# First keys placed from two queues, and the second group's queries and keys made after the first scores

## The chip, the cores and the metric

The kernel runs on one core of one Trainium2 chip. The metric is device microseconds of one execution. The engines are PE (TensorE: matmuls, and PEld for its weight loads), DVE (VectorE), ACT (ScalarE), POOL (GpSimd) and SP (SyncE, which only issues transfers). Each engine runs its own instructions in order and waits on semaphores; SP, ACT and POOL issue DMAs from their own queues.

## What is computed

A window-attention block followed by a gated depthwise-convolution block, on `x` of shape (8, 64, 32, 32), all in float32. The change touches only the start of the first block:

```python
xn = _layernorm(xc, ln1_scale, ln1_bias)              # over channels
qkv = xw @ w_qkv + b_qkv                              # windows of 8x8 pixels, 8 heads, depth 8
attn = jnp.einsum('bnhd,bmhd->bhnm', q * scale, k)
attn = attn + bias.transpose(2, 0, 1)[None]           # relative position bias from a small table
attn = jax.nn.softmax(attn, axis=-1)
out = jnp.einsum('bhnm,bmhd->bnhd', attn, v)
```

## The kernel before

The image columns are cut into NG = 8 groups of 512 columns (G), each NW = 8 windows. A group passes through these stages; the number in brackets is the line in the kernel before.

- The input is split into a high and a low part (`high_of_x`, `low_of_x` [L550, L287]), centred on PE (`centered` [L787]), squared on ACT (`square_of_centered` [L555, L556]), the square split again (`low_of_square` [L287]), averaged on PE (`variance` [L787]), turned into 1/deviation on ACT (`inverse_deviation` [L561, L563]) and multiplied in on DVE (`normalise` [L1194]).
- PE makes keys, queries and values (`keys` [L809], `queries` [L814], `values` [L819]). ACT evacuates their high parts (`evacuate_k` [L572], `evacuate_q` [L581]) and DVE makes the low parts (`k_low` [L1198], `q_low` [L1203]).
- The evacuated parts are spread by DMA into block layouts: `spread_keys` [L379] and `spread_queries` [L391] on SP, 8 DMAs each (the queries twice a group, one half after the other), and `first_key_blocks` [L453] and `query_blocks` [L469] on POOL, 4 DMAs each. `k_heads` and `q_heads` also hold rows of the position bias, written once: the keys' by `bias_with_keys` [L1172], the queries' early half by `bias_with_queries` [L1180] on DVE, the late half by `late_bias` [L675] on ACT. They come from two loaded tables, `rel_flipped` and `rel_table`, through `high_of_bias` [L1185] and `low_of_bias` [L1190].
- A first pass of products per window (`scores_for_max` [L840]) gives DVE the row maxima (`take_maximum` [L1216]), in three PSUM banks. They are transposed (`transpose_maxima` [L846]) and negated (`spread_maxima` [L1222 to L1225]); then `scores` [L864, L867] starts its sum with minus the maximum (through the constant `pick` [L435]), and ACT takes the exponentials (`exponentials` [L601]).

`step(g, ...)` holds the scores of group g, mixed with values and the pass for the maxima of the next group, and with centring, keys and queries of the one after. Ahead of `step(0)` each engine has a start-up written out by hand, and that is where the change lies. Nothing schedules the order: each engine's list is the order of the code, and semaphores tie the lists. SP's start-up is `spread_keys(0)`, both halves of `spread_queries(0)`, `spread_keys(1)`, four loads of `x`, and then 24 DMAs a group.

Of the kernel before, what the change touches and what calls it, by code (L numbers as in the profile page):

```python
# [7 lines left out]
WS, NH, HD = 8, 8, 8  # L8
# [90 lines left out]
def conv_seq_kernel(nc, d, out):  # L99
# [4 lines left out]
    with ctx:  # L104
# [105 lines left out]
        def gate_memory(space, nb):  # L210
# [22 lines left out]
            "ac_sq", "ac_log", "ac_rstd", "ac_q_high", "ac_k_high", "ac_v", "ac_probs", "ac_proj", "ac_sq2", "ac_log2", "ac_rstd2",   # L233
            "dv_normed", "dv_k_low", "dv_q_low", "k_heads_in", "q_blocked", "q_blocks_in", "k_blocked", "k_blocks_in", "q_heads_in0", "q_heads_in1", "dv_max", "dv_maxt", "dv_minus", "dv_turned", "dv_inv", "dv_ratios", "dv_att", "dv_x1", "dv_normed2",
            "pe_mlp1", "pe_mlp2", "pe_pw1", "ac_gelu", "ac_relu", "dv_x2", "dv_hsum",
# [94 lines left out]
        def query_rows(part, half, windows):  # L330
            rows = of_half(q_heads[:, part], half).rearrange("p h (w t) -> p h w t", t=T)
            return rows[:, :, windows.start:windows.stop, :]

        QUADRANTS = [(hh, bh, slice(hh * 64 + bh * 32, hh * 64 + bh * 32 + 32)) for hh in range(2) for bh in range(2)]

# [4 lines left out]
        def _(sp):  # L340
# [25 lines left out]

            def of_head(t, h):
                first = h // (NH // 2) * 64 + h % (NH // 2)
                return t[first:first + 64 - NH // 2 + 1:NH // 2]
# [12 lines left out]
            def spread_queries(n, half):  # L382

                if n == 0:
                    sp.wait_ge(S[f"q_heads_set{half}"], 1 + half)
# [44 lines left out]
        def _(pool):  # L430
            pool.memset(k_blocks[:, :, :, 1].bitcast(F32).rearrange("p h s w t -> p (h s) (w t)"), 0.0).then_inc(S["k_blocks_zeroed"], 1)
            pool.memset(gaps[:], 0.0).then_inc(S["zeroed"], 1)
            pool.wait_ge(S["consts_in"], 16)
            pool.wait_ge(S["center_in"], 16)
            pool.tensor_tensor(pick[:], const("average").unsqueeze(1).to_broadcast([128, NW, 128]),  # L435
# [11 lines left out]
            def first_key_blocks():  # L447

                pool.wait_ge(S["k_blocks_zeroed"], 1)
                pool.wait_ge(S["k_blocks_set"], 1)  # L450
                pool.wait_ge(S["dv_k_low"], 1)
# [32 lines left out]

            low_of_next_x(1)
            first_key_blocks()
            low_of_next_square(1)
# [44 lines left out]
        def _(act):  # L532
# [32 lines left out]
            def evacuate_k(n, par):  # L565
                act.wait_ge(S["pe_k"], n + 1)
                if not (isinstance(n, int) and n < 2):
                    act.wait_ge(S["k_heads_in"], 16 * NH * (n - 1))
                    act.wait_ge(S["k_blocks_in"], 64 * (n - 1))
# [85 lines left out]
            act.wait_ge(S["eps_set"], 1)  # L655
            act.dma_start(weights[:, _WAT["vec"][1]:], d["weights"][:, _WAT["vec"][1]:]).then_inc(S["weights_in"], 16)
            inverse_deviation(0)
            act.wait_ge(S["consts_in"], 16)
            for half in range(2):
                ins = act.activation(k_blocks[:, half, :, 0], reversal().rearrange("p (s w) t -> p s w t", s=2), ACT.Copy, scale=not_in_half(half))  # L660
            ins.then_inc(S["k_blocks_set"], 1)
            act.wait_ge(S["x_in0"], 32)
            high_of_x(1)
            act.wait_ge(S["qkv_ready"], 1)
            evacuate_k(0, 0)
            evacuate_q(0, 0)
# [5 lines left out]
            def late_bias(part, rel):  # L672
                late = range(NW // 2, NW)
                for half in range(2):
                    ins = act.activation(query_rows(part, half, late), bias_rows(rel, half, late), ACT.Copy, scale=not_in_half(half))  # L675
                ins.then_inc(S["q_heads_set1"], 1)

            act.wait_ge(S["dv_rel_low"], 1)
            late_bias(0, rel_high)
            inverse_deviation(1)  # L680
            act.wait_ge(S["x_in1"], 32)
            high_of_x(2)
            late_bias(1, rel_low)
            evacuate_q(1, 1)
            evacuate_k(1, 1)
            act.wait_ge(S["weights_ready"], 1)
# [96 lines left out]
        def _(pe):  # L783
# [39 lines left out]
            def scores_for_max(n, w):  # L823

                if w == 0:
                    if isinstance(n, int) and n == 0:
                        pe.wait_ge(S["q_blocked"], 1)
                    else:
                        pe.wait_ge(S["q_blocks_in"], 64 * n)
                    pe.wait_ge(S["k_heads_in"], 16 * NH * (n + 1))  # L830
                elif w == 1:
# [83 lines left out]
            def step(g, nxt, far, prev, par):  # L915
# [4 lines left out]

                scores(g, 0)
                if nxt is not None:
                    values(nxt)
# [39 lines left out]
            queries(0)  # L963
            values(0)
# [3 lines left out]
            pe.matmul(psum[:, PV, 5:6], proj_raw, qkv_bias[:, 2:3], start=True, stop=True).then_inc(S["pe_biases"], 1)  # L968
            centered(1)
# [161 lines left out]
        def _(dve):  # L1131
# [481 lines left out]
```

## Time and profile before

| | |
|---|---|
| median of 3 runs | 326.47 us (326.3 to 327.18) |
| profiled execution, its own time | 329.44 us |
| its span, first to last instruction | 327.6 us |
| busy: PE, DVE, ACT, POOL | 289.0 us (88%), 246.9 (75%), 203.0 (62%), 92.0 (28%) |
| chain that ended last, shares | PE 61%, DVE 12%, SP's queue 9%, ACT 6%, DMA 4% |
| one maximum on DVE (L1216), mean of 64 | 682 ns |

The chain is followed back from the last instruction, at each step to what released it; an engine busy outside of it costs nothing.

### The profile page before, as it was taken

The page shows a single profiled execution, that of the slowest core. Times are in us where ns is not written, and L with a number is a line of the kernel's source. Part 1 is how long each engine was busy: PE and PEld are TensorE (multiplying, and loading weights), DVE is VectorE, ACT ScalarE, POOL GpSimd, SP SyncE. Part 2 cuts the span into 40 slices and gives each one's busy share as a digit, 9 for nine tenths or more (in the row PEclk, how much of TensorE's full clock was granted, in tenths as well). Part 3 has the DMA queues.
Part 4 walks back from the last instruction along what each step waited for, and adds up shares of the span by engine and source line. Part 5 has one row for each costly group of instructions (what it writes and reads, how often), then busy time and mean ns, then how long its engine had stood idle before and what let it go on. Part 6 is the DMA issues. An engine that isn't in the chain of part 4 may idle for free.

```text
span 327.6 us, 6201 instructions
## 1 busy us (share of the span) xinstructions
PE 289.0 (88%) x2314; PEld 209.9 (64%) x2314; DVE 246.9 (75%) x484; ACT 203.0 (62%) x343; POOL 92.0 (28%) x116
## 2 busy tenths in 40 slices
PE   0577897989999898999979897899899999999994
PEld 0345684768868687776868653354477777777772
DVE  3686589579899898989977354779999999976211
ACT  5587643838658585765735697977961755754500
POOL 4063316255263464534250611131310000000000
PEclk9995999999999999999998999999999999999998
DMA  6961356224132331413320000392007568766911
GB/s 152 179 141 44 79 138 119 57 73 89 34 90 63 72 75 36 103 55 71 74 73 13 2 1 2 65 211 58 0 2 145 126 129 179 142 139 144 191 32 32
DMA packets 16380, 28.10 MB, mean 86 GB/s; under 512 B 5088, under 2 KB 11744, under 8 KB 16352
## 3 DMA queue, kind: packets, MB, share of 16 engines
q1 hardware_dynamic: 13792, 22.72, 30.5%
q0 software_dynamic: 1984, 4.20, 7.3%
q10 hardware_dynamic: 576, 0.81, 1.0%
q8 instruction: 18, 0.29, 0.4%
q14 instruction: 10, 0.08, 0.1%
HBM read 4.22 MB, written 2.10 MB: 19 GB/s over the span
## 4 chain that ended last, share of the span: by engine, by line
PE 61%; DVE 12%; SPq 9%; ACT 6%; DMA 4%; issue 4%; POOL 2%; DVEq 0%; ACTq 0%
PE psum L1088 26%; PE psum L867 8%; SPq L391 5%; PE psum L787 5%; SPq L379 4%; PE psum L1012 3%; DVE maxima L1216 3%; PE psum L864 3%; PE psum L1000 3%; DMA k_heads<-k_parts 3%; POOL parts L287 2%; PE psum L809 2%; PE psum L840 2%; PE psum L883 2%; DVE k_blocks L1210 2%
## 5 line engine op out<-in xcount | busy, mean ns | idle before, releaser
L1088 PE MATMUL psum<-shifted,conv_w 128*128 128x512 f32 x336 | 86.6, 419 | 0.0
L1088 PEld LDWEIGHTS psum<-shifted,conv_w 128*128 128x128 f32 x336 | 63.9, 191 | 21.5 <-issue 1.3
L867 PEld LDWEIGHTS psum<-q_heads,k_blocks 128*128 128x128 f32 x384 | 55.4, 191 | 5.9 <-issue 2.8
L867 PE MATMUL psum<-q_heads,k_blocks 128*128 128x256 f32 x384 | 56.6, 283 | 0.0
L1216 DVE TENSOR_REDUCE maxima<-psum 128x8 f32<-128x512 f32 x64 | 40.4, 682 | 11.1 <-PE psum L840 10.0
L601 ACT ACTIVATE probs<-psum 128x512 f32<-128x512 f32 x64 | 37.4, 603 | 15.8 <-PE psum L867 15.6
L287 POOL TENSOR_TENSOR parts<-x,parts 128x256 fp32r<-128x256 f32 (+1 forms) x21 | 19.4, 938 | 59.2 <-ACT parts L609 33.7
L787 PE MATMUL psum<-parts,center_average 128*128 128x512 f32 x64 | 23.1, 443 | 13.7 <-DVE parts L287 9.4
L864 PE MATMUL psum<-minus_max,pick 128*128 128x512 f32 x64 | 32.3, 504 | 2.4 <-DMA q_heads<-q_parts 1.9
L840 PE MATMUL psum<-k_heads,q_blocks 128*128 128x256 f32 x128 | 23.3, 308 | 8.1 <-DMA k_heads<-k_parts 5.5
L273 ACT CAST conv_w<-conv_w 32x896 fp32r<-32x896 f32 x31 | 29.1, 938 | 0.4
L1476 DVE SCALAR_TENSOR_TENSOR x<-psum,weights,x 64x512 f32<-64x512 f32 x16 | 12.0, 749 | 21.0 <-PE psum L1088 20.9
L287 POOL TENSOR_TENSOR parts<-square_logvar,parts 128x512 fp32r<-128x512 f32 x14 | 18.0, 1287 | 31.3 <-ACT square_logvar L556 16.0
L840 PEld LDWEIGHTS psum<-k_heads,q_blocks 128*128 128x128 f32 x128 | 19.4, 204 | 11.6 <-issue 6.3
L730 ACT CAST conv_w<-whole_w 128x896 fp32r<-128x896 f32 x8 | 7.5, 936 | 27.5 <-DVE whole_w L1451 18.9
L514 POOL TENSOR_TENSOR images<-square_logvar,images 128x512 fp32r<-128x512 f32 x8 | 10.7, 1339 | 42.0 <-ACT images L713 42.0
L787 PEld LDWEIGHTS psum<-parts,center_average 128*128 128x128 f32 x64 | 10.4, 200 | 17.0 <-issue 9.6
L703 ACT ACTIVATE hidden<-psum,mlp_bias 128x512 f32<-128x512 f32 x32 | 19.5, 699 | 2.5 <-PE psum L1000 2.4
L1000 PE MATMUL psum<-normed,mlp_w 128*128 128x512 f32 x64 | 18.4, 425 | 1.4 <-ACT hidden L703 1.4
L883 PEld LDWEIGHTS psum<-probs,v_blocks 128*32 128x32 f32 x1024 | 15.5, 112 | 5.2 <-issue 4.9
L1210 DVE CAST k_blocks<-k_parts 32x512 fp32r<-32x512 f32 x28 | 12.9, 459 | 7.4 <-PE psum L867 7.0
L461 POOL DMA_DIRECT2D k_blocks<-k_parts x28 | 16.1, 583 | 7.4 <-PE psum L867 6.8
(143 smaller groups left out, 486.9 us busy)
## 6 DMA issues: line engine op xcount, KB each, us to landing
shifted<-images SPq DMA_DIRECT2D x32, 332.5 KB, 5.5
q_heads<-q_parts SPq DMA_DIRECT2D x128, 32.0 KB, 1.8
k_heads<-k_parts SPq DMA_DIRECT2D x64, 32.0 KB, 2.3
out<-x SPq DMA_DIRECT2D x8, 256.0 KB, 4.9
q_blocks<-q_parts POOLq DMA_DIRECT2D x28, 64.0 KB, 2.5
k_blocks<-k_parts POOLq DMA_DIRECT2D x28, 64.0 KB
x<-in_x SPq DMA_DIRECT2D x6, 256.0 KB, 5.1
x<-in_x SPq DMA_DIRECT2D x4, 128.0 KB, 4.8
```

The costliest lines, as they stand in the source:

```text
L273: ins = copy(conv_w[bh][shift * KS:(shift + 1) * KS, part, :, C:], w[(shift - 1) * KS:shift * KS, :, 0:C])
L287: return engine.tensor_tensor(low, whole, high.bitcast(F32), ALU.subtract)
L601: act.activation(probs[:, w, :], psum[:, PROB0 + w % 2, :], ACT.Exp).then_inc(S["ac_probs"], 1)
L703: act.activation(hidden[:, par, m, :], psum[:, HIDDEN0 + m, :], ACT.Gelu, bias=mlp1_bias[:, m % 2:m % 2 + 1]).then_inc(S["ac_gelu"], 1)
L787: ins = pe.matmul(psum[:, bank, :], center_average[:, which, :], parts[:, part, :], start=part == 0, stop=part == 1)
L840: ins = pe.matmul(max_bank(w)[:, hh * G // 2:(hh + 1) * G // 2], q_blocks[:, hh, w, :], of_half(k_heads, hh)[:, :, w * T:(w + 1) * T], sta ...
L864: pe.matmul(bank, pick[:, w, :], minus_max[:, :, :], start=True, stop=False)
L867: ins = pe.matmul(bank[:, hh * G // 2:(hh + 1) * G // 2], k_blocks[:, hh, w // (NW // 2), k_part, w % (NW // 2), :], of_half(q_heads[:, q_ ...
L883: ins = pe.matmul(psum[32 * j:32 * j + 32, PV, column:column + T], v_blocks[:, par, at:at + 32], probs[:, w, head * T:(head + 1) * T], sta ...
L1000: ins = pe.matmul(psum[:, HIDDEN0 + m, :], mlp1_w[:, part, f * 128:(f + 1) * 128], normed2[:, bh, bass.ds(n * G, G)], start=part == 0, sto ...
L1088: ins = pe.matmul(psum[:, CONV0 + bh, :], conv_w[bh][:, w_part, t, :], img[:, y:y + H - 1:2, x0:x0 + W], start=t == 0 and w_part + part == ...
L1216: dve.tensor_reduce(maxima[:, w * NH:(w + 1) * NH], max_bank(w).rearrange("p (h t) -> p h t", t=T), AX.X, ALU.max).then_inc(S["dv_max"], 1)
```

## The change

It makes six moves, all at the start.

1. `spread_keys(0)` issues only heads 0 to 3 on SP; POOL issues heads 4 to 7, ahead of `first_key_blocks`, under a semaphore of its own. PE and ACT wait for both.
2. POOL makes `pick` after the first centring on PE and no longer as soon as the constants are in.
3. On DVE, `high_of_bias(1, rel_high)` stands ahead of `normalise(0)`; both biases and both low parts stand before the maxima, with the queries' first, and `other_weights` too; `normalise(1)` stands behind all eight maxima.
4. On ACT, the two halves of the key blocks' constants stand on either side of `inverse_deviation(0)`, one of the four late bias copies ahead of `evacuate_q(0)` and the other three ahead of `inverse_deviation(1)`.
5. On PE, the small bias products stand ahead of `values(0)`, and `variance(1)` behind the sixth window of the first maximum pass instead of the second.
6. `queries(1)` and `keys(1)` are no longer made around `transpose_maxima(0)` but in `step(0)`, behind `scores(0, 0)`; ACT evacuates them behind the first exponential.

```diff
-                for h in range(NH):
-                    sp.dma_start(of_head(k_heads, h)[:, h, :].bitcast(F32).rearrange("p (s c) -> p s c", s=2),
-                                 of_head(k_parts, h)[:, n % 2, :, 0, :].bitcast(F32)).then_inc(S["k_heads_in"], 16)
+                for h in FIRST_KEYS_BY_SP if n == 0 else range(NH):
+                    keys_of_head(sp, n, h, "k_heads_in")
...
             pool.wait_ge(S["consts_in"], 16)
-            pool.wait_ge(S["center_in"], 16)
+            pool.wait_ge(S["pe_xc"], 1)
...
             low_of_next_x(1)
+            pool.wait_ge(S["ac_k_high"], 1)
+            pool.wait_ge(S["k_heads_set"], 1)
+            for h in FIRST_KEYS_BY_POOL:
+                keys_of_head(pool, 0, h, "first_keys_in")
             first_key_blocks()
...
                 exponentials(g, 0)
+                if isinstance(g, int) and g == 0:
+                    evacuate_q(1, 1)
+                    evacuate_k(1, 1)
...
             for w in range(NW):
                 scores_for_max(0, w)
-                if w == 1:
+                if w == 5:
                     variance(1)
-            pe.wait_ge(S["dv_normed"], 2)
-            queries(1)
             transpose_maxima(0)
-            keys(1)
...
             high_of_bias(0, rel_flipped, "dv_rel_flipped")
+            high_of_bias(1, rel_high, "dv_rel_high")
             normalise(0)
             bias_with_keys()
+            low_of_bias()
+            bias_with_queries()
+            q_low(0, 0)
             k_low(0, 0)
-            high_of_bias(1, rel_high, "dv_rel_high")
-            low_of_bias()
-            q_low(0, 0)
-            bias_with_queries()
+            other_weights()
             for w in range(NW):
                 take_maximum(0, w)
-                if w == 3:
-                    normalise(1)
             spread_maxima(0)
-            other_weights()
+            normalise(1)
```

`high_of_bias` waits for its table (`dve.wait_ge(S[f"rel_in{n}"], 32)`) before it copies.

The order on DVE at the start, in the kernel before, from `q_blocks`' constants to the first maxima:

```order
L1167 TENSOR_SCALAR q_blocks<-consts 128x1024 x2
L1185 CAST normed<-probs 128x512
L1194 TENSOR_TENSOR normed<-psum,rstd 128x512
L1172 TENSOR_SCALAR k_heads<-normed,consts 128x2048 x2
L1198 SCALAR_TENSOR_TENSOR k_parts<-psum,qkv_bias,k_parts 128x2x256
L1185 CAST normed<-probs 128x512
L1190 TENSOR_TENSOR normed<-probs,normed 128x512
L1203 SCALAR_TENSOR_TENSOR q_parts<-psum,q_bias,q_parts 128x512
L1180 TENSOR_SCALAR q_heads<-normed,consts 128x4x256 x4
L1216 TENSOR_REDUCE maxima<-psum 128x8 x4
L1194 TENSOR_TENSOR normed<-psum,rstd 128x512
```

The same place on DVE in the changed kernel (L1204 is the copy of a table, L1213 `normalise`, L1222 `q_low`, L1217 `k_low`, L1235 the maxima):

```order
L1186 TENSOR_SCALAR q_blocks<-consts 128x1024 x2
L1204 CAST normed<-probs 128x512 x2
L1213 TENSOR_TENSOR normed<-psum,rstd 128x512
L1191 TENSOR_SCALAR k_heads<-normed,consts 128x2048 x2
L1209 TENSOR_TENSOR normed<-probs,normed 128x512
L1199 TENSOR_SCALAR q_heads<-normed,consts 128x4x256 x4
L1222 SCALAR_TENSOR_TENSOR q_parts<-psum,q_bias,q_parts 128x512
L1217 SCALAR_TENSOR_TENSOR k_parts<-psum,qkv_bias,k_parts 128x2x256
```

Both table copies now stand ahead of the first normalisation, and `k_low` has moved from behind the key bias to behind the query bias.

The order on PE in the kernel before, from the centring of the second group (L787) to the first scores (L864, L867):

```order
L787 MATMUL psum<-parts,center_average 128x512 x2
L840 MATMUL psum<-k_heads,q_blocks 128x256 x4
L787 MATMUL psum<-parts,center_average 128x512 x2
L840 MATMUL psum<-k_heads,q_blocks 128x256 x12
L814 MATMUL psum<-normed,qkv_w 128x512
L846 MATMUL psum<-consts,maxima 64x128
L809 MATMUL psum<-normed,qkv_w 128x512
L864 MATMUL psum<-minus_max,pick 128x512
L867 MATMUL psum<-q_heads,k_blocks 128x256 x6
```

The same place on PE in the changed kernel (L858 is the maximum pass, L864 the transpose, L882 and L885 the scores, L832 and L827 queries and keys):

```order
L805 MATMUL psum<-parts,center_average 128x512 x2
L858 MATMUL psum<-k_heads,q_blocks 128x256 x12
L805 MATMUL psum<-parts,center_average 128x512 x2
L858 MATMUL psum<-k_heads,q_blocks 128x256 x4
L864 MATMUL psum<-consts,maxima 64x128
L882 MATMUL psum<-minus_max,pick 128x512
L885 MATMUL psum<-q_heads,k_blocks 128x256 x6
L832 MATMUL psum<-normed,qkv_w 128x512
L827 MATMUL psum<-normed,qkv_w 128x512
```

The variance has moved from behind two windows to behind six, and queries and keys from ahead of the first scores to behind them.

## Rows read from the trace of the kernel before

**Rows 1.** Timeline of PE: start us, us, engine line operation, xcount [idle before, releaser]

```profile
15.21 2.05 PE L809 MATMUL psum<-normed,qkv_w 128*128 128x512 f32 x2 [2.33 <-DVE normed L1194]
...
26.51 1.20 PE L840 MATMUL psum<-k_heads,q_blocks 128*128 128x256 f32 x4 [4.17 <-DMA k_heads<-k_parts]
27.50 1.05 PE L787 MATMUL psum<-parts,center_average 128*128 128x512 f32 x2
...
33.35 0.43 PE L846 MATMUL psum<-consts,maxima 128*64 128x128 f32 x2 [0.43 <-DVE maxima L1216]
...
35.10 0.47 PE L864 MATMUL psum<-minus_max,pick 128*128 128x512 f32 x1 [0.26 <-issue]
...
49.92 1.10 PE L809 MATMUL psum<-normed,qkv_w 128*128 128x512 f32 x2 [0.19 <-DVE maxima L1216]
...
55.42 0.47 PE L864 MATMUL psum<-minus_max,pick 128*128 128x512 f32 x1 [1.88 <-DMA q_heads<-q_parts]
```

**Rows 2.** Timeline of SP, its DMA issues

```profile
32.67 5.10 SPq L391 DMA_DIRECT2D q_heads<-q_parts  x8
37.86 5.90 SPq L379 DMA_DIRECT2D k_heads<-k_parts  x8
...
46.41 11.37 SPq L391 DMA_DIRECT2D q_heads<-q_parts  x16
```

**Rows 3.** Source line L343 in the window 4 to 6: the second loads of x

```profile
L343 SPq DMA_DIRECT2D x<-in_x x2: 534/565/596, 4.2 to 4.7; - x2
...
DMA to landing us min/median/max: 5.7/6.5/7.2
```

**Rows 4.** Source line L362: the load of the raw weights on SP

```profile
L362 SPq DMA_DIRECT2D probs<-in_raw x1: 560/560/560, 6.7 to 6.7; - x1
...
DMA to landing us min/median/max: 11.3/11.3/11.3
```

**Rows 5.** DMA queue of ACT: packets, MB, share, windows 15:16 and 16:17

```profile
q10 hardware_dynamic: 3, 0.00, 0.3%
...
q10 hardware_dynamic: 29, 0.10, 28.6%
```

**Rows 6.** Timeline of DVE

```profile
5.96 2.46 DVE L287 TENSOR_TENSOR parts<-x,parts 128x256 fp32r<-128x256 f32 x2
...
13.22 0.61 DVE L1185 CAST normed<-probs 128x512 fp32r<-128x512 f32 x1
14.37 0.69 DVE L1194 TENSOR_TENSOR normed<-psum,rstd 128x512 f32<-128x512 f32 x1 [0.53 <-ACT rstd L563]
14.97 2.47 DVE L1172 TENSOR_SCALAR k_heads<-normed,consts 128x2048 fp32r<-128x2048 f32 x2
...
19.39 1.08 DVE L1190 TENSOR_TENSOR normed<-probs,normed 128x512 fp32r<-128x512 f32 x1
...
21.06 2.88 DVE L1180 TENSOR_SCALAR q_heads<-normed,consts 128x1024 fp32r<-128x1024 f32 x4
...
36.10 0.74 DVE L1203 SCALAR_TENSOR_TENSOR q_parts<-psum,q_bias,q_parts 128x512 fp32r<-128x512 f32 x1
```

**Rows 7.** Timeline of POOL

```profile
6.24 1.90 POOL L435 TENSOR_TENSOR pick<-consts 128x1024 fp32r<-128x1024 f32 x1 [3.63 <-DMA consts<-in_consts]
...
19.56 3.23 POOL L453 DMA_DIRECT2D k_blocks<-k_parts  x4 [0.85 <-DVE k_parts L1198]
24.97 1.26 POOL L287 TENSOR_TENSOR parts<-square_logvar,parts 128x512 fp32r<-128x512 f32 x1 [2.18 <-ACT square_logvar L556]
```

**Rows 8.** Timeline of ACT

```profile
17.35 0.69 ACT L572 ACTIVATE k_parts<-psum,qkv_bias 128x512 fp32r<-128x512 f32 x1 [0.41 <-PE psum L809]
```

**Rows 9.** Stretch, PE, PEld, DVE, ACT, POOL busy, PEclk, DMA, GB/s

```profile
24.00:26.00 2.00, 0.00 (x0) 0.00 (x0) 0.00 (x0) 1.98 (x4) 1.03 (x1) 0.64 0.56 105
```

**Rows 10.** Chain that ended last, in order of time: start us, us, what

```profile
172.67 0.73 PE psum L864
173.40 1.28 PE psum L867 x6
174.68 0.32 PE psum L864
175.00 0.71 PE psum L867 x6
```

More of the change, by code:

```diff
@@ L332, in query_rows, with of_head, keys_of_head, wait_keys_placed @@
             return rows[:, :, windows.start:windows.stop, :]
+        def of_head(t, h):
+            first = h // (NH // 2) * 64 + h % (NH // 2)
+            return t[first:first + 64 - NH // 2 + 1:NH // 2]
+        def keys_of_head(engine, n, h, done):
+            engine.dma_start(of_head(k_heads, h)[:, h, :].bitcast(F32).rearrange("p (s c) -> p s c", s=2),
+                             of_head(k_parts, h)[:, n % 2, :, 0, :].bitcast(F32)).then_inc(S[done], 16)
+        FIRST_KEYS_BY_SP, FIRST_KEYS_BY_POOL = range(0, NH // 2), range(NH // 2, NH)
+        def wait_keys_placed(engine, groups):
+            engine.wait_ge(S["k_heads_in"], 16 * (NH * groups - len(FIRST_KEYS_BY_POOL)))
+            engine.wait_ge(S["first_keys_in"], 16 * len(FIRST_KEYS_BY_POOL))
         QUADRANTS = [(hh, bh, slice(hh * 64 + bh * 32, hh * 64 + bh * 32 + 32)) for hh in range(2) for bh in range(2)]
@@ L363, in _ @@
             load_x(1, slice(0, PIX), S["x_in1"])
-            def of_head(t, h):
-                first = h // (NH // 2) * 64 + h % (NH // 2)
-                return t[first:first + 64 - NH // 2 + 1:NH // 2]
             def spread_keys(n):
@@ L377, in spread_keys @@
                     sp.wait_ge(S["pe_max"], NW * n)
-                for h in range(NH):
-                    sp.dma_start(of_head(k_heads, h)[:, h, :].bitcast(F32).rearrange("p (s c) -> p s c", s=2),
-                                 of_head(k_parts, h)[:, n % 2, :, 0, :].bitcast(F32)).then_inc(S["k_heads_in"], 16)
+                for h in FIRST_KEYS_BY_SP if n == 0 else range(NH):
+                    keys_of_head(sp, n, h, "k_heads_in")
             def spread_queries(n, half):
                 if n == 0:
-                    sp.wait_ge(S[f"q_heads_set{half}"], 1 + half)
+                    sp.wait_ge(S[f"q_heads_set{half}"], 1 + 3 * half)
                 else:
@@ L449, in first_key_blocks @@
                 pool.wait_ge(S["k_blocks_zeroed"], 1)
-                pool.wait_ge(S["k_blocks_set"], 1)
+                pool.wait_ge(S["k_blocks_set"], 2)
                 pool.wait_ge(S["dv_k_low"], 1)
@@ L567, in evacuate_k @@
                 if not (isinstance(n, int) and n < 2):
-                    act.wait_ge(S["k_heads_in"], 16 * NH * (n - 1))
+                    wait_keys_placed(act, n - 1)
                     act.wait_ge(S["k_blocks_in"], 64 * (n - 1))
@@ L656, in _, with key_block_constants, late_bias @@
             act.dma_start(weights[:, _WAT["vec"][1]:], d["weights"][:, _WAT["vec"][1]:]).then_inc(S["weights_in"], 16)
+            def key_block_constants(half):
+                act.activation(k_blocks[:, half, :, 0], reversal().rearrange("p (s w) t -> p s w t", s=2), ACT.Copy, scale=not_in_half(half)
+                               ).then_inc(S["k_blocks_set"], 1)
+            def late_bias(part, rel, half):
+                late = range(NW // 2, NW)
+                act.activation(query_rows(part, half, late), bias_rows(rel, half, late), ACT.Copy, scale=not_in_half(half)
+                               ).then_inc(S["q_heads_set1"], 1)
+            act.wait_ge(S["consts_in"], 16)
+            key_block_constants(0)
             inverse_deviation(0)
[L658 to L661, printed above, removed]
+            key_block_constants(1)
             act.wait_ge(S["x_in0"], 32)
@@ L665, in _ @@
             evacuate_k(0, 0)
+            act.wait_ge(S["dv_rel_high"], 1)
+            late_bias(0, rel_high, 0)
             evacuate_q(0, 0)
@@ L670, in _ @@
             square_of_centered(1)
[L672 to L676, printed above, removed]
+            late_bias(0, rel_high, 1)
             act.wait_ge(S["dv_rel_low"], 1)
-            late_bias(0, rel_high)
+            for half in range(2):
+                late_bias(1, rel_low, half)
             inverse_deviation(1)
@@ L682, in _ @@
             high_of_x(2)
-            late_bias(1, rel_low)
-            evacuate_q(1, 1)
-            evacuate_k(1, 1)
             act.wait_ge(S["weights_ready"], 1)
@@ L829, in scores_for_max @@
                         pe.wait_ge(S["q_blocks_in"], 64 * n)
-                    pe.wait_ge(S["k_heads_in"], 16 * NH * (n + 1))
+                    wait_keys_placed(pe, n + 1)
                 elif w == 1:
@@ L921, in step @@
                 scores(g, 0)
+                if isinstance(g, int) and g == 0:
+                    pe.wait_ge(S["dv_normed"], 2)
+                    queries(1)
+                    keys(1)
                 if nxt is not None:
@@ L963, in _ @@
             queries(0)
-            values(0)
             pe.wait_ge(S["raw_in"], 16)
@@ L968, in _ @@
             pe.matmul(psum[:, PV, 5:6], proj_raw, qkv_bias[:, 2:3], start=True, stop=True).then_inc(S["pe_biases"], 1)
+            values(0)
             centered(1)
```

2 lines of the change are left out of this document (1 added, 1 removed).

## The prediction, on record before the changed kernel ran

> **What bounds the kernel now.** I read four views, in this order. The page's chain shows PE for most of the span, so from the middle on the kernel is a PE-led rhythm that this change does not touch; it can only shift it. The chain in order of time then shows that from about 33 to 66 us the shift is set by SP's queue. In its timeline [rows 2] the second half of the first queries is issued from 32.67, the second group's keys from 37.86 and the next 16 queries from 46.41, each block right behind the last (four loads of x stand between the last two). PE's timeline shows who waits for it: at 55.42 it had been idle 1.88 us for q_heads [rows 1]. So the quantity to follow is when SP begins the second group's keys: 37.86 before. What leads up to it is PE's 4.17 us wait for the first keys until 26.51, the transpose of the maxima at 33.35 and the first scores at 35.10 [rows 1]. Last, DVE's timeline shows the start-up's own chain: table copy at 13.22, `normalise(0)` at 14.37, PE's keys at 15.21 [rows 1, 6].
>
> **The table copy ahead of `normalise(0)`.** This edit decides the case. `high_of_bias(1)` waits for rel_table, and DVE is in order, so `normalise(0)` and all behind it wait too. Before, that copy stood late and nothing shows a wait. The landing itself has no row, so I bound it. SP issues rel_table after the second loads of x and before the raw weights. The former was issued last at 4.7 and took up to 7.2: 11.9 us [rows 3]. The latter was issued at 6.7 and took 11.3: 18.0 us [rows 4]. In between, ACT's queue moved 3 packets from 15 to 16 us and 29 from 16 to 17 [rows 5]: something in front of it on the crowded DMA engines was over at about 16, and only rel_table's large rows and the raw weights stood there. I take 16.5, nearer the later bound. The copy costs 0.6 [rows 6], so `normalise(0)` starts at 17.15 and not at 14.37: 2.8 us late. PE's keys go from 15.21 to 18.0.
>
> **What that hides.** Moving `pick` off the start helps: DVE's split of the first x took 2.46 us for two halves while POOL ran `pick` from 6.24 for 1.90 [rows 6, 7], some 1.6 us more than two undisturbed halves by my estimate. The first centring comes that much earlier, but `normalise(0)` then waits for the table anyway: worth 0 at a landing of 16.5, and about 1.0 were the table there. The Trainium skill, SBUF — State Buffer, section SBUF: two separate sides, has DVE and GpSimd share a port pair as an exclusive lock that the first to start holds for its whole instruction. The trace agrees with it in these two rows, and by it the moved `pick` meets the low part of the first square instead, which is why I count 1.0 and not 1.6 there. The key-block constant put ahead of `inverse_deviation(0)` lies in ACT's wait for the variance: 0.
>
> **From `normalise(0)` to the transpose.** DVE now runs without a gap: normalise 0.69, key bias 2.47, low of the table 1.08, query bias 2.88, `q_low` and `k_low` 0.74 each [rows 6], less five overlaps of some 0.06: `k_low` ends at 25.4. Behind it POOL issues the four key-block DMAs, 3.23 us, and only then splits the second square, 1.26 [rows 7]: with 0.3 to start, 30.2. PE has `variance(1)` behind window 5, so it waits until then, takes 0.9 to 1.05, and windows 6 and 7 queue behind it at 0.6 each [rows 1], with a maximum of 0.68 behind each. The transpose T comes at 30.2 + 0.9 + 0.7 + 2 x 0.68 = 33.2, against 33.35. DVE's own eight maxima, begun at about 26.6 behind `other_weights`, would be over by 32.1, so they do not set it. The first keys, the wait of 4.17, are thus moved earlier against their own start, since four issues leave SP, but what they release is not late any more; the gain is given back to the table. If PE's clock is at its full level here, T is 32.6 (lower bound); if the key-block DMAs take the short 0.6 each, 0.5 earlier still.
>
> **From the transpose to SP.** Before, the scores came 1.75 us behind T [rows 1]. Now queries and keys are behind them. At full clock the scores take 1.03 [rows 10], queries 1.03, keys 1.10 [rows 1], ACT's evacuation 0.7 [rows 8] and the handover 0.05: SP can start the second keys at T + 5.65 = 38.85. SP is free by then (the late bias copies end at about 31, its half of the queries takes 5.10 [rows 2]: 36.2). Against 37.86 that is 1.0 late. The removed work does not come back as gain: queries and keys took the wait for `spread_maxima` before, and now cost some 2.1 us between the first scores and the rest of step 0. PE's path there arrives 1.9 us late at the second maximum pass, but had 1.88 us of idle at 55.42 in front of the next scores [rows 1], so SP's 1.0 rules. Behind 66 us everything shifts alike. Edits of which I see no effect: the bias products ahead of `values(0)` (ACT is still copying query blocks), `other_weights` (hidden behind the first landing), POOL's four DMAs if they land by 27.
>
> The sum is +1.0 us. Against the profiled execution, 329.44 us with a span of 327.6, that is 330.4; its own time lies 3 us above the median of the runs, and the same +1.0 on 326.47 gives 327.5.
>
> **Rivals.**
> 1. *The table lands early: faster.* Each microsecond that it lands earlier moves T and SP alike. Break-even is 15.5 us. At 12.9 or before, where the deviation is ready, the whole design works: T at about 29.5, SP at 35.15, 2.7 us gained, 323.8. For it: over half of the range between the two landings [rows 3, 4] lies below 15.5. Against: the packets of ACT's queue [rows 5]. ACT now issues its large load some 1.6 us earlier too, which can only delay it. Chance 0.15.
> 2. *PE's clock falls in front of the first scores: clearly slower.* Before, PE stood idle 4.17 us and the granted clock went to 0.64 of a stretch in which it did nothing [rows 9], so that the pass ran at 1.2 GHz; queries and keys then kept it busy up to the scores. Now they are gone from there: between the variance and the scores PE has two windows and a transpose, under 2 us of work in 4. At the lower level the six score matmuls take 1.28 for 0.71 [rows 10] and the keys 2.05 for 1.10 [rows 1]. For scores, queries and keys that makes +0.6 +0.9 +0.95 = 2.4, straight onto SP's start: +3.4, 329.9. Against it: PE was idle 1.88 us at 55.42 and its scores then took 0.47 as before [rows 1]. Chance 0.27. The Trainium skill, TensorE: Matmul & The Clock Gate, section What's actually happening, says that the monitor runs free of the kernel; by that rule the same gap costs in some executions and not in others. No row here shows that.
> 3. *POOL's key DMAs starve.* They are issued while DVE runs the long bias operations; POOL's issues took 0.8 each in that state [rows 7]. If the last head lands at 28.5 and not at 26, the eight maxima set T, at about 34: 328.2. Chance 0.09. The Trainium skill, SBUF — State Buffer, section A bandwidth-pool intuition that's wrong, has GpSimd unable to write descriptors while DVE holds the pair, and this rule speaks against placing them there; the first key blocks, issued beside such operations before, fit it loosely.
>
> **How the numbers follow.** My forecast is 327.5, chance 0.47, with its own range 326.6 to 328.2 (a table at 16.0 to 17.0, and T at 32.6 to 33.7). About 0.3%, 1.0 us, is what a measurement can tell here, so this case lies on the border: 0.24 within, 0.23 slower. Rival 1: 0.12 faster, 0.03 within. Rival 2: slower, 0.27. Rival 3: slower 0.04, within 0.05. A small gain from a short key-block issue at full clock has 0.02, faster. That makes 0.14 faster, 0.32 within and 0.54 slower. The range 326.0 to 330.2 leaves out the table well early and a clock that is low for longer.
>
> **What would show it.** DVE idle for some 3.5 us until about 16.5, released by a DMA, ahead of the second table copy; `normalise(0)` at 17.2; PE's keys at 18.0; the small wait of PE for the first keys (under 1 us for the former 4.17); PE waiting for POOL's split ahead of window 6; the transpose at 33; SP's second keys at 38.9. Wrong would be: a DVE that does not wait before the copy; a clock under 1 between 33 and 38; or a maximum pass that waits for POOL's heads.

## The result, and the profile after

The changed kernel takes 331.42 us (median of 4 runs, 329.6 to 333.06) against 326.83 us for the kernel before on the same chip (4 runs, 326.3 to 327.39). The ratio is 1.0151, interval 1.0119 to 1.0183: 4.6 us slower. The forecast was 327.5, at most 330.2. The profiled execution took 330.42 us, 1.0 us below its own median, while the one of before was 3 us above its.

The page of the changed kernel, its span and the chain that ended last by engine:

```profile
span 328.6 us, 6204 instructions
...
PE 59%; DVE 21%; issue 6%; ACT 5%; POOL 4%; DMA 3%; SPq 1%; DVEq 0%; POOLq 0%
```

SP's queue had 9% of the chain before and has 1% now. The chain in order of time says what took its place, from the start of the trace up to the second group's queries:

```profile
6.06 8.80 DMA probs<-in_rel_table
14.95 0.91 DVE normed L1204
15.88 0.69 DVE normed L1213
16.57 2.39 DVE k_heads L1191 x2
...
24.59 2.60 POOL k_blocks L462 x4
27.21 1.30 POOL parts L287
28.55 1.22 PE psum L805 x2
...
31.58 0.69 PE psum L864 x2
32.27 1.61 issue
33.88 0.76 PE psum L882
34.64 1.28 PE psum L885 x6
35.92 1.71 PE psum L832 x2
37.63 1.51 PE psum L827 x2
```

This is the path that the prediction drew: the load of rel_table, DVE's copy and `normalise(0)`, POOL's key blocks and second square, the second variance, the transpose. Behind the transpose, though, each matmul has the long one of its two durations. DVE's timeline has the wait and its price:

```profile
8.83 1.44 DVE L287 TENSOR_TENSOR parts<-square_logvar,parts 128x512 fp32r<-128x512 f32 x1 [2.03 <-ACT square_logvar L569]
...
14.95 0.89 DVE L1204 CAST normed<-probs 128x512 fp32r<-128x512 f32 x1 [2.45 <-DMA probs<-in_rel_table]
```

The timeline of POOL; its second row is the four heads of keys that it took over from SP:

```profile
7.83 1.90 POOL L444 TENSOR_TENSOR pick<-consts 128x1024 fp32r<-128x1024 f32 x1 [5.22 <-PE psum L805]
...
19.86 2.84 POOL L339 DMA_DIRECT2D k_heads<-k_parts  x4 [3.42 <-ACT k_parts L585]
```

The timeline of PE (compare [rows 1]): the first keys, the maximum pass, the transpose, the first scores, and the second group's queries and keys.

```profile
16.72 2.05 PE L827 MATMUL psum<-normed,qkv_w 128*128 128x512 f32 x2 [5.17 <-DVE normed L1213]
...
24.49 0.63 PE L858 MATMUL psum<-k_heads,q_blocks 128*128 128x256 f32 x2
25.53 0.97 PE L858 MATMUL psum<-k_heads,q_blocks 128*128 128x256 f32 x6 [0.41 <-ACT v_blocks L609]
...
31.58 0.69 PE L864 MATMUL psum<-consts,maxima 128*64 128x128 f32 x2 [0.95 <-DVE maxima L1235]
33.88 0.76 PE L882 MATMUL psum<-minus_max,pick 128*128 128x512 f32 x1 [1.61 <-issue]
34.44 1.48 PE L885 MATMUL psum<-q_heads,k_blocks 128*128 128x256 f32 x6
35.72 1.91 PE L832 MATMUL psum<-normed,qkv_w 128*128 128x512 f32 x2
37.42 1.72 PE L827 MATMUL psum<-normed,qkv_w 128*128 128x512 f32 x2
```

The maximum pass begins at 24.49 without a wait, where PE waited 4.17 us until 26.51 before. Stretches of two microseconds (columns as in [rows 9], the granted clock stands ahead of the last two):

```profile
28.00:30.00 2.00, 1.45 (x5) 1.26 (x6) 1.15 (x2) 2.00 (x3) 0.49 (x1) 0.64 0.68 173
30.00:32.00 2.00, 1.04 (x5) 0.62 (x4) 1.29 (x2) 1.72 (x4) 0.17 (x1) 0.50 0.16 50
32.00:34.00 2.00, 0.39 (x3) 0.15 (x1) 1.65 (x4) 0.00 (x0) 1.23 (x2) 0.50 0.15 49
...
36.00:38.00 2.00, 2.00 (x3) 0.73 (x3) 0.00 (x0) 0.93 (x2) 0.00 (x0) 0.50 0.04 14
38.00:40.00 2.00, 2.00 (x11) 1.36 (x10) 0.85 (x2) 1.04 (x2) 1.35 (x3) 0.80 0.19 33
40.00:42.00 2.00, 2.00 (x16) 1.83 (x15) 0.65 (x1) 1.84 (x5) 0.96 (x2) 1.00 0.65 118
```

The granted clock is 0.5, the lower level of 1.2 GHz, through the scores, the queries and most of the keys. The mean of 0.64 in the stretch from 28 to 30 puts the fall at about 28.6, by estimate. Ahead of it PE had waited 0.41 us for ACT, 0.31 for DVE's maxima and 0.63 for POOL's split; the longer waits around the transpose, 0.95 and 1.61, came behind the fall. SP's timeline gives the second group's keys at 39.89, against 37.86 before [rows 2]:

```profile
39.89 5.00 SPq L339 DMA_DIRECT2D k_heads<-k_parts  x8
```

### The profile page after: what moved, and what is told of

Same layout as the page of the kernel before. It is cut to its first block, busy times and chain, and to the rows that moved or that the text cites. A ratio compares the mean times of both kernels' runs of the same rounds, so it can differ in the third digit from the quotient of the medians.

```text
span 328.6 us, 6204 instructions
## 1 busy us (share of the span) xinstructions
PE 291.5 (89%) x2314; PEld 211.4 (64%) x2314; DVE 246.7 (75%) x484; ACT 202.9 (62%) x343; POOL 94.3 (29%) x120
## 4 chain that ended last, share of the span: by engine, by line
PE 59%; DVE 21%; issue 6%; ACT 5%; POOL 4%; DMA 3%; SPq 1%; DVEq 0%; POOLq 0%
PE psum L1107 26%; PE psum L885 7%; DVE maxima L1235 4%; PE psum L1031 3%; PE psum L805 3%; POOL parts L287 3%; PE psum L882 3%; PE psum L1019 3%; DMA probs<-in_rel_table 3%; PE psum L827 2%; PE psum L901 2%; PE psum L858 2%; DVE k_blocks L1229 2%; DVE normed L287 2%; PE psum L1043 1%
## 5 line engine op out<-in xcount | busy, mean ns | idle before, releaser
L885 PEld LDWEIGHTS psum<-q_heads,k_blocks 128*128 128x128 f32 x384 | 55.8, 193 | 6.1 <-issue 2.6
L885 PE MATMUL psum<-q_heads,k_blocks 128*128 128x256 f32 x384 | 57.0, 285 | 0.0
L1235 DVE TENSOR_REDUCE maxima<-psum 128x8 f32<-128x512 f32 x64 | 40.4, 684 | 8.8 <-PE psum L858 7.7
L882 PE MATMUL psum<-minus_max,pick 128*128 128x512 f32 x64 | 32.6, 510 | 1.9 <-issue 1.6
L858 PE MATMUL psum<-k_heads,q_blocks 128*128 128x256 f32 x128 | 22.4, 298 | 4.5 <-DVE maxima L1235 2.5
L858 PEld LDWEIGHTS psum<-k_heads,q_blocks 128*128 128x128 f32 x128 | 18.7, 195 | 7.9 <-DVE maxima L1235 4.4
L805 PEld LDWEIGHTS psum<-parts,center_average 128*128 128x128 f32 x64 | 10.6, 204 | 16.5 <-issue 7.5
L478 POOL DMA_DIRECT2D q_blocks<-q_parts x28 | 16.2, 584 | 9.7 <-ACT q_parts L594 9.7
L901 PE MATMUL psum<-probs,v_blocks 128*32 128x64 f32 x1024 | 18.4, 226 | 0.0
```

Of the source, the lines that this page charges most:

```text
L805: ins = pe.matmul(psum[:, bank, :], center_average[:, which, :], parts[:, part, :], start=part == 0, stop=part == 1)
L858: ins = pe.matmul(max_bank(w)[:, hh * G // 2:(hh + 1) * G // 2], q_blocks[:, hh, w, :], of_half(k_heads, hh)[:, :, w * T:(w + 1) * T], sta ...
L882: pe.matmul(bank, pick[:, w, :], minus_max[:, :, :], start=True, stop=False)
L885: ins = pe.matmul(bank[:, hh * G // 2:(hh + 1) * G // 2], k_blocks[:, hh, w // (NW // 2), k_part, w % (NW // 2), :], of_half(q_heads[:, q_ ...
L901: ins = pe.matmul(psum[32 * j:32 * j + 32, PV, column:column + T], v_blocks[:, par, at:at + 32], probs[:, w, head * T:(head + 1) * T], sta ...
L1235: dve.tensor_reduce(maxima[:, w * NH:(w + 1) * NH], max_bank(w).rearrange("p (h t) -> p h t", t=T), AX.X, ALU.max).then_inc(S["dv_max"], 1)
```

## A marker for all traces

The third maximum pass (the first is the one of the start-up) begins with a group of four window matmuls, at 66.22 in the trace of before. Its start is called M here. "Falls" stands where the granted clock is under 1.00 somewhere from 164 to 180 us:

| kernel | M | profiled time | time − M | PE's clock 164 to 180 us |
|---|---|---|---|---|
| before | 66.22 | 329.44 | 263.22 | falls |
| before, again (e0) | 64.13 | 327.39 | 263.26 | falls |
| after | 67.14 | 330.42 | 263.28 | falls |
| e1 | 66.08 | 328.45 | 262.37 | full |
| e2 | 65.00 | 328.21 | 263.21 | falls |
| e3 | 64.39 | 326.85 | 262.46 | full |
| e4 | 69.65 | 332.03 | 262.38 | full |
| e5 | 65.79 | 329.06 | 263.27 | falls |
| e6 | 61.85 | 325.12 | 263.27 | falls |
| e7 | 64.27 | 326.70 | 262.43 | full |
| e8 | 64.64 | 327.92 | 263.28 | falls |
| e9 | 69.93 | 333.21 | 263.28 | falls |
| e10 | 63.07 | 326.32 | 263.25 | falls |
| e11 | 61.83 | 324.25 | 262.42 | full |

Whatever the edit, the rest takes 263.2 to 263.3 us, or 262.4 to 262.5 where the clock stays full late in the kernel. So everything that the edits do is done by M, and the later fall goes with 0.8 us more. One entry needs care: in e1 the granted clock reads 1.00 in every stretch, also where its matmuls take the long durations (below); late in the kernel they take the short ones (six score matmuls 0.88 from 172 to 178 us), and its 262.37 stands with the others called full.

## The experiments

Ratios are to the kernel before, run on the same chip; its medians there were 326.76, 326.42 and 326.55 us. Two theories were open: that the wait for rel_table costs the time, and that PE's low clock at the scores, queries and keys behind the transpose does. Each expectation says what it would see of its own.

**The kernel before, again** (no edit). 

> The kernel before, unchanged, for a second profile. The 4.6 us of the change are measured against runs of 326.8 us, but the profiled execution of before took 329.44. Theory A (that one profile was a late one: its loads ended at 20 us and the first keys landed 3.4 us behind their issue): here the first keys land within 2.5 us of their issue, PE's wait for them is under 3.5 us, and the profiled time is 326 to 327.5. Theory B (profiling adds it always): again 329 to 330, with PE's first maximum pass at 26.5 us.

326.37 us, ratio 0.9999 (0.998 to 1.0018). The profiled time, 327.39, is as theory A has it, but its two other signs did not come: PE waited 5.32 us for the first keys, and these landed up to 3.8 us behind their issue (3.6 in the trace of before). The difference lies elsewhere. Timeline of DVE, then of POOL, then of PE at the second group's scores:

```profile
6.53 0.76 DVE L287 TENSOR_TENSOR parts<-x,parts 128x256 fp32r<-128x256 f32 x2
...
13.25 0.69 DVE L1194 TENSOR_TENSOR normed<-psum,rstd 128x512 f32<-128x512 f32 x1 [0.54 <-ACT rstd L563]
```

```profile
7.50 2.00 POOL L435 TENSOR_TENSOR pick<-consts 128x1024 fp32r<-128x1024 f32 x1 [4.89 <-DMA consts<-in_consts]
```

```profile
52.99 0.47 PE L864 MATMUL psum<-minus_max,pick 128*128 128x512 f32 x1
```

Here POOL's `pick` starts behind DVE's split, and the split takes 0.76 us, not 2.46 [rows 6, 7]. `normalise(0)` stands at 13.25, not 14.37, and SP's second keys at 36.77, not 37.86: 1.1 us earlier. M is 2.1 us earlier. More than the earlier start shows in it: the wait of 1.88 us for q_heads at 55.42 [rows 1] is not there, and the same scores begin at 52.99, 2.4 us earlier, and wait for nothing.

**The table copy back behind the key bias, in the changed kernel.**

```diff
-            high_of_bias(1, rel_high, "dv_rel_high")
             normalise(0)
             bias_with_keys()
+            high_of_bias(1, rel_high, "dv_rel_high")
```

> The changed kernel with the copy of the second table back behind the key bias, all else as changed. If the wait for the table costs most of the loss (theory T), normalise(0) starts at about 13.2 us, everything up to the first scores comes 2 to 3 us earlier, and the time is 328 to 329. If the queries and keys behind the first scores cost it (theory Q), at most 1 us is gained: over 330.

329.03 us, 1.0083 (1.0057 to 1.0109): 2.2 us of the 4.9 of the ratio come back. The first scores come at 33.06, 0.8 us earlier and not 2 to 3 as expected, since the table landed later in this execution and DVE still waits 1.20 us for it, behind the key bias, until 17.40. The six score matmuls take 1.48 all the same, and SP's second keys stand at 39.27. The profile's granted clock contradicts these durations (stretch of 34 to 36 us):

```profile
34.00:36.00 2.00, 2.00 (x8) 1.48 (x7) 0.00 (x0) 0.60 (x1) 0.00 (x0) 1.00 0.10 33
```

The durations are taken as right here, since from the transpose to SP's second keys it takes 8.51 us, as slow as the changed kernel's 8.31.

**Queries and keys back around the transpose, in the changed kernel**, with `normalise(1)` behind the seventh maximum.

```diff
-                if isinstance(g, int) and g == 0:
-                    pe.wait_ge(S["dv_normed"], 2)
-                    queries(1)
-                    keys(1)
...
+            pe.wait_ge(S["dv_normed"], 2)
+            queries(1)
             transpose_maxima(0)
+            keys(1)
```

> The changed kernel with the second group's queries and keys back around the transpose, evacuated ahead of the step, and the second normalise ahead of the last maximum; the table copy stays early. Theory Q: SP starts the second keys some 3 us earlier (37 us), PE's clock does not fall in front of the first scores, and the time is 328 to 329. Theory T: 330 to 331, since the start is as late as in the changed kernel.

328.99 us, 1.0073 (1.0046 to 1.01): 2.5 us back. The table wait is still there (DVE idle 3.28 us until 16.24), and SP's second keys come at 37.88. The clock did fall in front of the scores, which was not expected: it is 0.50 from 34 to 36 us, and queries and keys take 1.55 and 2.05; the six score matmuls behind them take 0.88. So this run puts the two back into their place and does not hold the clock up; it does not part the two.

**Both repairs.** 

> Both repairs together. If T and Q each cost something and add, this is 325 to 327, at least the time before. If one of the two alone explains the loss, it equals the better of the two single repairs within 0.5 us. What is left of the change in it: the split of the first keys, the moved pick, constants, and the order of low parts.

326.74 us, 1.0003 (0.9975 to 1.0032). The two repairs add up and take back all. The granted clock is 0.50 here from 28 to 36 us too. What is left of the change (split keys, late `pick`, order of biases, constants and variance) is worth nothing together, although the split alone gains 2.3 us (e6); what eats its gain here was not tried.

**The table copy alone, in the kernel before.**

```diff
             high_of_bias(0, rel_flipped, "dv_rel_flipped")
+            high_of_bias(1, rel_high, "dv_rel_high")
             normalise(0)
             bias_with_keys()
             k_low(0, 0)
-            high_of_bias(1, rel_high, "dv_rel_high")
```

> The kernel before with one edit: the copy of the second table ahead of normalise(0). The table landed between 14.9 and 17.4 us in five profiles, and normalise(0) starts at 13.2 to 14.4 without it. Theory T: normalise(0) starts about 0.9 us behind the landing, 15.8 to 18.3, and the time rises by 1.5 to 2.5 us (factor 1.005 to 1.008). Rival (the start-up has slack): within 0.5 us of before.

330.81 us, 1.0126 (1.0095 to 1.0157): 4.1 us from one line, where 1.5 to 2.5 were expected. The timeline of DVE:

```profile
17.91 0.62 DVE L1185 CAST normed<-probs 128x512 fp32r<-128x512 f32 x1 [5.66 <-DMA probs<-in_rel_table]
18.57 0.69 DVE L1194 TENSOR_TENSOR normed<-psum,rstd 128x512 f32<-128x512 f32 x1
```

DVE stands 5.66 us for the table; `normalise(0)` is 5.3 us later than in e0, and SP's second keys 5.0 (41.81). The granted clock is 1.00 from 36 to 42 us, at the transpose and the first scores (six matmuls 0.88), so this price is the wait's and not the clock's.

**Queries and keys behind the first scores, alone, in the kernel before** (the edit of e2 the other way round; `normalise(1)` stays in its place). 

> The kernel before with one edit: the second group's queries and keys behind the first scores, evacuated behind the first exponential. Theory Q: SP starts the second keys 1.5 to 3 us later than the 36.8 to 37.9 of before, and the time rises by 1.5 to 2.5 us. Rival (queries and keys only change places with the wait for spread_maxima): within 0.5 us.

329.63 us, 1.0111 (1.0076 to 1.0146): 3.6 us, where again 1.5 to 2.5 were expected; between the profiled executions of e0 and of this run M shows 1.7 of it. The timeline of PE:

```profile
33.58 0.77 PE L865 MATMUL psum<-minus_max,pick 128*128 128x512 f32 x1 [1.31 <-issue]
34.14 1.48 PE L868 MATMUL psum<-q_heads,k_blocks 128*128 128x256 f32 x6
35.42 1.59 PE L815 MATMUL psum<-normed,qkv_w 128*128 128x512 f32 x2
```

The same slow scores, and slower queries (full speed is 1.02), without the rest of the change. PE had idled 1.29 us ahead of the transpose and 1.31 behind it.

**The split of the first keys alone, in the kernel before.**

```diff
-                for h in range(NH):
...
+                for h in FIRST_KEYS_BY_SP if n == 0 else range(NH):
+                    keys_of_head(sp, n, h, "k_heads_in")
...
+            for h in FIRST_KEYS_BY_POOL:
+                keys_of_head(pool, 0, h, "first_keys_in")
```

> The kernel before with one edit: the first keys of heads 4 to 7 issued by POOL. PE waits until 25.5 to 26.5 us for the first keys before. If SP's issues set that, the first maximum pass starts 1 to 2.5 us earlier and the time falls by up to 1.5 us. If POOL's descriptors are held up beside DVE's bias operations, or the four issues only push back POOL's key blocks and its split of the second square, it stays within 0.5 us or rises.

324.43 us, 0.9929 (0.9903 to 0.9955): 2.3 us faster, the lowest median of all runs. The timeline of PE:

```profile
22.18 0.71 PE L853 MATMUL psum<-k_heads,q_blocks 128*128 128x256 f32 x4 [1.54 <-DMA k_heads<-k_parts]
24.57 1.22 PE L800 MATMUL psum<-parts,center_average 128*128 128x512 f32 x2 [1.69 <-POOL parts L287]
```

The pass starts at 22.18, against 25.51 in e0. Part of the gain goes to a new wait for POOL, whose second square now stands behind eight DMAs; SP's second keys are 1.8 us earlier (35.00) and M 2.3.

**Filler matmuls in the changed kernel.** Matmuls whose product nobody reads keep PE busy where it waits; the rest of the work is unchanged.

```diff
+            def filler(columns):
+                pe.matmul(psum[:, PROB0 + 1, 0:columns], qkv_w[:, 0, :], consts[:, 0:columns], start=True, stop=True)
...
+            filler(512)
+            filler(512)
             keys(0)
...
                 scores_for_max(0, w)
+                if w == 0:
+                    filler(128)
                 if w == 5:
+                    filler(256)
                     variance(1)
+            filler(256)
             transpose_maxima(0)
+            filler(256)
+            filler(128)
```

> The changed kernel with added matmuls on PE whose results nobody reads: two of 512 columns in the wait ahead of the first keys, and 128 to 384 columns in the gaps between the first maximum windows and the first scores. Theory C (a low clock of PE at the scores, queries and keys is what makes their new place dear): the granted clock is 1.00 there, L-keys take 1.1 and not 1.7 to 2.0 us, SP starts the second keys 1.5 to 2.5 us earlier than 39.9, and the time falls by 1 to 2 us. Rival (the place itself costs, at any clock): within 0.5 us of the changed kernel.

326.72 us, 1.0007 (0.9986 to 1.0028): 4.7 us come back with no instruction moved, where 1 to 2 were expected. The timelines of DVE and of PE:

```profile
16.98 0.61 DVE L1217 CAST normed<-probs 128x512 fp32r<-128x512 f32 x1 [3.94 <-DMA probs<-in_rel_table]
```

```profile
32.64 0.43 PE L864 MATMUL psum<-consts,maxima 128*64 128x128 f32 x2 [0.71 <-DVE maxima L1248]
33.00 0.92 PE L976 MATMUL psum<-consts,qkv_w 128*128 128x256 f32 x4
34.45 0.47 PE L882 MATMUL psum<-minus_max,pick 128*128 128x512 f32 x1 [0.53 <-issue]
...
35.47 1.02 PE L832 MATMUL psum<-normed,qkv_w 128*128 128x512 f32 x2
36.33 1.02 PE L827 MATMUL psum<-normed,qkv_w 128*128 128x512 f32 x2
```

From the transpose to SP's second keys (38.10) it takes 5.46 us, against 8.31 in the changed kernel: 2.85. By the starts of the rows, 0.49 of it lie between the transpose and the scores, 0.82 in the scores, 0.84 in the queries and 0.70 from the keys to SP. The table came 2.03 later here and the transpose only 1.06, so some 1.0 was won ahead of it as well, and 1.1 behind SP's second keys (26.17 us from there to M, against 27.25). M is 2.9 earlier, and with the 0.8 of the later fall that is absent the two profiled executions differ by 3.7. The medians differ by 4.7: the changed kernel's trace has the earliest table and lies 1.0 below its median. How the rest of the 4.7 is made up was not tried.

**`pick` behind the first centring, alone, in the kernel before.**

```diff
-            pool.wait_ge(S["center_in"], 16)
+            pool.wait_ge(S["pe_xc"], 1)
```

> The kernel before with one edit: pick behind the first centring. In the profile of before POOL's pick began at 6.24 us and held up DVE's split of the first x; in four later profiles the constants landed later, the split was over by 6.9 us, and with the late pick the first square's low part took 1.44 for 0.69 us. So theory P: the edit costs about 0.7 us in most executions (326.5 to 327.6). Rival (the collision of that first profile is the usual state): it gains up to 1.5 us.

327.36 us, 1.0012 (0.999 to 1.0034): no gain, perhaps 0.4 us lost. DVE's and POOL's timelines:

```profile
9.25 1.44 DVE L287 TENSOR_TENSOR parts<-square_logvar,parts 128x512 fp32r<-128x512 f32 x1 [2.03 <-ACT square_logvar L556]
```

```profile
8.25 1.89 POOL L435 TENSOR_TENSOR pick<-consts 128x1024 fp32r<-128x1024 f32 x1 [5.64 <-PE psum L787]
```

The low part of the first square takes 1.44 us beside `pick`; in e0 it took 0.69.

**The load of the table ahead of the other bias and of the second x, in the changed kernel.** 

> The changed kernel, all orders as they are, but SP issues the second bias table ahead of the first one and of the second loads of x. If the loss is the wait for that table's landing and not the place of the copy itself, DVE's wait in front of it goes from 2.5 to 5.7 us to under 1, and the time falls by about as much as with the copy placed late (2.4 us): 328.5 to 329.5. Rival: the table that is loaded second now lands as late as the other did, the wait only moves to the other copy, and the time stays at 331.

331.8 us, 1.0145 (1.0108 to 1.0181), as the changed kernel and as the rival has it. The timeline of DVE:

```profile
17.00 1.27 DVE L1204 CAST normed<-probs 128x512 fp32r<-128x512 f32 x2 [4.49 <-DMA probs<-in_rel_flipped]
```

The same wait, now for the other table, until 17.00.

**Filler matmuls in the kernel before** (384 columns ahead of the first keys, three of 512 in the wait for `k_heads`). 

> The kernel before with matmuls nobody reads: 384 columns in front of the first keys, and three of 512 columns in PE's wait for the spread first keys. With fillers the changed kernel fell by 4.7 us. If a low clock costs every order of this start-up alike, before falls by 3 us or more as well. Theory C (the low clock is dear where queries and keys stand behind the first scores, on the way to SP): before falls by at most 1.5 us, since its queries and keys lie beside the wait for the maxima.

325.79 us, 0.9974 (0.9945 to 1.0003): 0.8 us, not told from nothing. From 17 us on the matmuls take the short one of their durations, the six score matmuls 0.88, and M came 1.1 earlier than in e0. So PE's low clock is cheap in the kernel before and dear in the changed kernel.

**The split, `variance(1)` behind the fourth window, and fillers** (384, 384 and 128 columns). 

> The kernel before with the split of the first keys (324.4 us alone), variance(1) behind window 3 and no longer 1 (PE waited 1.7 us there for POOL's split of the square), and fillers of 384, 384 and 128 columns. If the wait and the clock are what is left at that place, SP starts the second keys 1 to 2 us earlier than 35.0, and the time is 323 to 324. Rival: DVE's maxima or SP's own queue of first queries set it, and it stays at 324.4.

324.49 us, 0.9941 (0.992 to 0.9962), as the split alone, so the rival holds. M is 61.83 against 61.85. PE waits 2.05 us for DVE's maxima ahead of the last window.

## Why the prediction was wrong

Each part was foreseen, and the time was not. Two steps failed: the sum took the path from the transpose to SP at full clock, T + 5.65, where it measured 8.31 (step 6 below), and it was made on one long execution and carried over to the median (step 2). By the prediction's own steps:

1. **The table copy.** Right in kind: DVE waits for rel_table, released by a DMA, and the landing estimate of 16.5 stands among the 16.24, 16.98, 17.21, 17.40 and 17.91 at which a wait for it ended in e2, e7, e11, e1 and e4. The changed kernel's own trace has 14.95, the earliest. The **size was wrong because of the base**: 17.15 was set against a `normalise(0)` at 14.37, which this one trace had because `pick` met the split. In e0 it stands at 13.25. The term is +3.9 against that, not +2.8, and the edit alone measured 4.1 us (e4).
2. **"The same +1.0 on 326.47."** This step failed. The sum came from an execution 3 us above the median and was carried over to the median unchanged. Against e0 that execution is 2.1 us late at M: 1.1 us of it are there at `normalise(0)` already (`pick` beside the split), and it has the wait of 1.88 us for q_heads, which e0 has not. The late `normalise(0)` also hides a wait that ends at the table's landing. Against the profiled execution the sum gave 330.4, and 330.42 was measured, but by luck: the table was 1.6 us early, and the clock was low.
3. **The wait hides the rest: `pick` worth 0.** Right: 1.0012 alone. The six other traces with `pick` in its old place have no collision with the split to remove (in e4, e6 and e10 `pick` meets a scaling of weights behind it, 1.95 to 2.01 us for 0.28 or 0.35, which is over before the square is there), and with `pick` late a new one with the square is made (1.44 for 0.69), as the prediction had read from the Trainium skill, SBUF — State Buffer, section SBUF: two separate sides. The trace agrees: the row of 7.83 to 9.73 on POOL overlaps that of 8.83 on DVE.
4. **From `normalise(0)` to the transpose.** 16.05 us were foreseen; 15.70 it took in the changed kernel (15.88 to 31.58), 15.01 with fillers. Right.
5. **Rival 3, starved key DMAs.** Not seen in the changed kernel: four issues beside DVE's bias operations took 2.84 us, 0.71 each (SP's four 2.57, 0.64 each), and the pass began without waiting for a key. In e7 and e9 the four took 3.13 and 3.11 us, and PE waited 0.58 and 1.77 us for keys. What the prediction cited from the Trainium skill, SBUF — State Buffer, section A bandwidth-pool intuition that's wrong, does not show in these issues as a stop for the length of a DVE operation.
6. **From the transpose to SP, T + 5.65.** 5.46 in e7 at the full clock, so the path was right. In the changed kernel it was 8.31, since **rival 2 came true**: 2.66 more, where it was priced at 2.4. The price had left out the first matmul of the scores, 0.73 for 0.32 in [rows 10]. It was given a chance of 0.27; in all four traces with queries and keys behind the scores and no filler (after, e1, e5, e9) the six score matmuls took 1.48 to 1.49. It belonged in the sum. The evidence against it was an idle of 1.88 us at 55.42 that cost no clock. In the changed kernel the clock fell behind three shorter waits (0.41, 0.31 and 0.63 us); why these cost it and the longer one did not is not shown. The clock was low around the transpose in e0 too (its queries took 1.91), and full there in e10, which moved M by 1.1 only: in e0 queries and keys stand in front of the scores, and the six score matmuls took 0.88 already.
7. **SP's 1.0 rules, PE's own path has 1.88 us to spare.** Wrong with the slow clock: the chain leaves SP (1% of it, from 9%) and stays on PE. At 55.95 PE's scores wait for nothing. M is then +3.0 against e0. The 1.88 us was no fixed reserve either: it is 0 in e0, 1.08 in e8 and 1.60 in e10.
8. **Behind 66 us everything shifts alike.** Right, to 0.1 us (the table of M).

Put together from e0 and not from the trace of before: SP's second keys at the forecast 38.85 are 2.1 late, not 1.0, and rival 2's 2.4 makes 4.5, on 326.47 331.0, against 331.42 measured. That is worked out afterwards, and e0's own execution still lies 1.0 above the median. The two causes were measured apart: the repairs of e1 (2.2) and e2 (2.5) sum to about e3 (4.8). But the fillers of e7 give 4.7 back with the table's wait still there, and from the other side the single edits give +4.1 +3.6 −2.3 +0.4 = +5.8 for 4.9. So the prices do not simply add; which of them overlap was not tried.

**Left open**: why the clock late in the kernel falls in some traces (0.8 us); why the stretch from SP's second keys to M takes 26.2 us in e7 and 28.4 in the trace of before, with the others between; how much the moved queries and keys would cost at the full clock with the table repaired, which was not run; and how the table's landing is spread over executions (14.95 to 17.91 in the six traces that have it as the end of a wait). That this spread makes the one of the changed kernel's runs, 329.6 to 333.06, is not shown.

## What to carry to other kernels

Before a sum is made on one profiled execution, compare its time with the median: if it is far off, take a second profile, find what made the first one long, and ask whether a wait that ends at a fixed time gets longer when that is gone. A copy put in front of critical work on an in-order engine makes that work wait for the copy's operand, however short the copy is; put it behind. Work moved out of a gap on PE can have two prices, its new place and the clock at which what follows runs: here the split alone gains 2.3 us, and the two moves beside it lose 4.1 and 3.6.

## What was not expected of the hardware

- Putting rel_table first only made the other table the late one: DVE waited until 17.00 for rel_flipped (e9), whose copy had begun at 11.89 without a wait in the changed kernel.
- Fillers in PE's waits are worth 4.7 us in the changed kernel and some 0.8, not told from nothing, in the kernel before.
- In e1 the profile's granted clock is 1.00 throughout while the matmuls from the transpose to the second group's keys take the long durations. In the changed kernel it is 1.00 from 16 to 20 us, where the two matmuls of the first keys take the long 2.05. The granted clock has to be read together with the durations.
- The late fall of the clock comes and goes. The Trainium skill, TensorE: Matmul & The Clock Gate, section What's actually happening, has the monitor of the clock run free of the kernel. The traces fit it loosely: late in the kernel the same work runs at the full clock in five traces and not in nine. Stretch of 168 to 172 us in e0 and in e7, where 0.57 and 1.00 are the granted clock:

```profile
168.00:172.00 4.00, 4.00 (x71) 2.82 (x72) 3.22 (x9) 1.32 (x2) 1.01 (x2) 0.57 0.47 103
```

```profile
168.00:172.00 4.00, 3.93 (x81) 3.21 (x82) 3.36 (x10) 1.92 (x3) 1.17 (x3) 1.00 0.52 111
```
